# Two six-layer stacks: the last four bodies as one sequence with the turns of the results inside, and a shorter list of entry work

## The reference

```
x = x + 0.5 * _L2_ffn_ref(_layernorm(x), Wqkv, q_scale, k_scale, Wo, ln_g, ln_b, W1, b1, W2, b2)
x = x + _L2_attn_ref(_layernorm(x), ...)
x = x + 0.5 * _L2_ffn_ref(_layernorm(x), ...)

for layer in range(6):                       # _L2_ffn_ref, on z
    t = shift_tokens(z)                      # the upper 64 features come from the token before
    q, k, v = split(t @ Wqkv[layer])         # 16 heads of 64
    q, k = rotary(l2norm(q) * q_scale), rotary(l2norm(k) * k_scale)
    a = softmax(8 * q @ k.T over a window of 32 keys back) @ v
    z = z + a @ Wo[layer]
    n = layer_norm(z) * ln_g + ln_b
    z = z + (u * gelu(g)) @ W2 + b2          # u, g = split(n @ W1 + b1), 341 wide each
```

## Time and profile before

| | us |
|---|---|
| runs | 5355.53, 5368.52, 5376.36; median 5368.52 |
| the profiled execution | 5368.35, its span 5366.6 |
| first stack, entry to last x | about 1018 to 2768 |
| second stack | about 3004 to 4768 |
| from output(46) to output(47), first stack | 27.6 |
| from output(47) to the last x | 28.8 |

### The profile page before, as it was taken

One profiled execution on the slowest core, in us unless ns is written; L12 is line 12 of the kernel. 1 busy time (PEld: TensorE's weight loads), 2 busy tenths in 40 slices (PEclk: granted clock), 3 DMA queues, 4 the chain that ended last, 5 costly groups with the idle time before them and its releaser, 6 DMA issues. The chain is left out here.

```text
span 5366.6 us, 141783 instructions
## 1 busy us (share of the span) xinstructions
PE 4978.9 (93%) x49044; PEld 3454.0 (64%) x49044; DVE 3814.0 (71%) x7030; ACT 3438.1 (64%) x5879; POOL 2867.6 (53%) x3451
## 2 busy tenths in 40 slices
PE   8988977499999999999969699999999999989889
PEld 5655655267777777777745367777777777756556
DVE  2243236488888888888856488888888888845545
ACT  3333323278888888888845378888888888832642
POOL 0010005378788778778720288777787787700200
PEclk9989988599999999999979799999999999989899
DMA  1000000011111111112100111111111111110000
GB/s 44 1 5 34 1 1 9 29 45 55 51 50 51 55 51 49 51 51 55 43 15 1 40 39 55 51 51 49 55 51 55 46 55 51 39 34 7 1 25 9
DMA packets 110454, 195.51 MB, mean 36 GB/s; under 512 B 21409, under 2 KB 28849, under 8 KB 110257
## 3 DMA queue, kind: packets, MB, share of 16 engines
q1 hardware_dynamic: 110256, 192.82, 12.8%
HBM read 53.29 MB, written 1.05 MB: 10 GB/s over the span
## 5 line engine op out<-in xcount | busy, mean ns | idle before, releaser
L2674 POOL TENSOR_TENSOR stage_qk<-stage_halves 128x1024 f32<-128x1024 f32 x384 | 906.0, 2359 | 53.3 <-DVE stage_halves L2790 45.8
L2710 POOL TENSOR_TENSOR stage_qk<-stage_qk,stage_rnorm 128x1024 f32<-128x1024 f32 x384 | 730.9, 1903 | 30.5 <-issue 0.3
L2703 POOL TENSOR_TENSOR stage_probs<-stage_probs,stage_rsum 128x768 f32<-128x768 f32 x384 | 565.3, 1472 | 222.1 <-DVE stage_rsum L2819 209.6
L2787 DVE TENSOR_TENSOR stage_halves<-stage_wide,stage_tables 128x1024 f32<-128x1024 f32 x384 | 468.2, 1219 | 227.6 <-ACT stage_square L2493 187.4
L2493 ACT ACTIVATE stage_square<-stage_wide 128x1024 f32<-128x1024 f32 x384 | 394.0, 1026 | 191.9 <-PE stage_wide L2259 191.5
L2325 PE MATMUL stage_pv<-stage_probsT,stage_v_win 96*64 96x64 f32 x12288 | 488.1, 227 | 2.7 <-ACT stage_ctxT L2546 1.6
L2790 DVE TENSOR_TENSOR stage_halves<-stage_wide,stage_tables 128x512 f32<-128x512 f32 x768 | 490.5, 680 | 0.0
L2325 PEld LDWEIGHTS stage_pv<-stage_probsT,stage_v_win 96*64 96x64 f32 x12288 | 408.4, 137 | 122.7 <-issue 98.5
L2799 DVE TENSOR_REDUCE stage_norm<-stage_square 128x16 f32<-128x1024 f32 x384 | 464.7, 1210 | 30.8 <-issue 30.7
L2276 PE MATMUL stage_turn<-ident,stage_qk 128*128 128x128 f32 x3072 | 478.9, 279 | 4.9 <-ACT stage_qkT L2513 4.7
L2311 PEld LDWEIGHTS stage_flip<-ident,stage_probs 128*96 128x96 f32 x3072 | 355.6, 126 | 194.3 <-issue 130.0
(11 more groups left out here) (299 smaller groups left out, 9877.6 us busy)
## 6 DMA issues: line engine op xcount, KB each, us to landing
stage_v_win<-stage_v SPq DMA_DIRECT2D x384, 192.0 KB, 2.5
stage_v_win<-stage_v SPq DMA_DIRECT2D x384, 128.0 KB, 2.4
stage_v_win<-stage_v SPq DMA_DIRECT2D x192, 64.0 KB, 2.2
stage_wq<-in_T_wq SPq DMA_DIRECT2D x12, 512.0 KB, 4.1
stage_wk<-in_T_wk SPq DMA_DIRECT2D x12, 512.0 KB, 4.7
stage_wv<-in_T_wv SPq DMA_DIRECT2D x12, 512.0 KB, 3.5
stage_wo<-in_T_wo SPq DMA_DIRECT2D x12, 512.0 KB, 3.5
stage_w_up<-in_L_w_up SPq DMA_DIRECT2D x8, 512.0 KB, 6.6
```

What stands on the lines that cost most here:

```text
L2674: nc.gpsimd.tensor_tensor(qk[:, n, :], halves[:, n % 2, 0, :], halves[:, n % 2, 1, :], ALU.add)\
L2703: nc.gpsimd.tensor_tensor(probs[:, m % 2], probs[:, m % 2], rsum[:, m % 2].to_broadcast([P, 2, 2 * HALVES, REACH]), ALU.mult)\
L2710: nc.gpsimd.tensor_tensor(heads, heads, rnorm[:, n, :].rearrange("p (h o) -> p h o", o=1).to_broadcast([P, LH, LD]), ALU.mult).then_inc(at ...
L2787: nc.vector.tensor_tensor(out[:, 0], heads, cos.to_broadcast([P, LH, LD]), ALU.mult)
```

## The change

In the entry, v_win is set only in its first 32 rows of block 0 (32 x 1024, to 0.0), DVE makes only the table of layer 0, and the activation table for exp and ln is loaded at the head of the entry instead of the head of the main block. The tables of layers 1 to 5 are made by POOL at the head of its main list; DVE waits for them in front of its loop. At the end, the calls of `body` for 46 to 49 and the loop over the eight batches are replaced by one written list per engine, `tail()`, in which the parts of steps 45 to 47 stand in another order and the turns of the results between them: `straighten(b)` on ACT, `turn_out(b)` on PE, `leave(b)` on DVE. `straight` now lies in `square`, and the transposes go to the banks of `wide`.

```diff
-        straight = qk[:, 2, :].rearrange("p (a s) -> p a s", s=SEQ)
+        straight = square[:, 0, :].rearrange("p (a s) -> p a s", s=SEQ)
...
-                nc.gpsimd.memset(v_win[:, :, :, :], 1.0).then_inc(once["set"], 1)
+                nc.gpsimd.memset(v_win[0:WINDOW, 0, :, :], 0.0).then_inc(once["set"], 1)
...
             @block.scalar
             def _(act):
+                nc.scalar.preload_act_table_set("natural_log_exp_and_others")
...
-                for layer in range(DEPTH):
-                    table(layer)
-                dve.wait_ge(*once("tables", 1))
+                table(0)
+                dve.wait_ge(*once("tables", 0, 1))
...
+            def turn_out(b):
+                if b == 0:
+                    pe.wait_ge(*att("v", STEPS - 1, HALVES))
+                pe.wait_ge(att["leave"], att.base["leave"] + b + 1)
+                if b > 1:
+                    pe.wait_ge(att["left"], att.base["left"] + b - 1)
+                for t in range(HALVES):
+                    ins = nc.tensor.transpose(wide[:, b % 2, t * P:(t + 1) * P], straight[:, b % 4, t * P:(t + 1) * P], chip.ident[:, :])
+                ins.then_inc(att["tok"], 1)
...
+            def tail():
+                fourth, third, second, last = range(STEPS - 4, STEPS)
+                project(last, 5)
+                weigh(second, 0)
...
-            for s in range(STEPS - 2, STEPS + 2):
-                body(s)
-            for b in range(B):
...
+            tail()
...
+            def straighten(b):
+                if b == 0:
+                    act.wait_ge(*att("norm2", STEPS - 1, CHUNKS))
+                act.wait_ge(*att("z", STEPS + b + 1))
+                if b > 3:
+                    act.wait_ge(att["tok"], att.base["tok"] + B + b - 3)
+                nc.scalar.activation(straight[low, b % 4, :], z[low, b, 0:SEQ], ACT.Copy)
+                nc.scalar.activation(straight[high, b % 4, :], z[high, b, 1:SEQ + 1], ACT.Copy).then_inc(att["leave"], 1)
...
+            for layer in range(1, DEPTH):
+                nc.gpsimd.tensor_tensor(tables[:, layer], base[:, :, :, :], rows[:, layer].to_broadcast([P, 4, HALVES, LD]), ALU.mult)\
+                  .then_inc(once["tables"], 1)
...
+            def leave(b):
+                dve.wait_ge(att["tok"], att.base["tok"] + B + b + 1)
+                x = chip.x[:, b * HALVES:(b + 1) * HALVES, :]
+                nc.vector.scalar_tensor_tensor(x, tiles2(wide[:, b % 2, :]), 0.5, x, ALU.mult, ALU.add).then_inc(att["left"], 1)
...
             for s in range(-2, 2):
                 body(s)
+            dve.wait_ge(*once("tables", 1))
             att.settle(dve)
             with dve.Fori(2, STEPS - 2) as s:
                 body(s)
```

More of the change, by code:

```diff
@@ L2470, in _ @@
                 body(s)
-            for s in range(STEPS - 2, STEPS + 2):
-                body(s)
-            for b in range(B):
-                pe.wait_ge(att["leave"], att.base["leave"] + b + 1)
-                if b > 1:
-                    pe.wait_ge(att["left"], att.base["left"] + b - 1)
-                bank = (flip, turn)[b % 2]
-                for t in range(HALVES):
-                    ins = nc.tensor.transpose(bank[:, t * P:(t + 1) * P], straight[:, b % 4, t * P:(t + 1) * P], chip.ident[:, :])
-                ins.then_inc(att["tok"], 1)
+            tail()
         @block.scalar
```

216 lines of the change are left out of this document (200 added, 16 removed).

## The result

The changed kernel takes 5337.96 us (median of 9 runs, 5328.03 to 5348.02), the kernel before 5371.79 us (median of 9, 5354.6 to 5376.36): 33.8 us less, a ratio of 0.9945 with a 95% interval of 0.9932 to 0.9958. The forecast was 5332.8 us in a range of 5318 to 5348, so the time lies inside it, 5.2 us above the forecast. The profiled execution took 5331.61 us at a span of 5329.8, 36.8 us less than the span of before, with a mean granted clock of 0.953.

The account below looks back on a forecast made before the run. It saw PE with hardly a gap in the loop, the drain bound by engine-to-engine waits. Entry 5.7, drain 7.5, output(47) 1.8 and turns 2.8 make 17.8 us a stack, 35.6 off 5368.4: 5332.8 us, range 5318 to 5348.

Parts of the forecast that it names:

- Entry: Start of each stack: shorter memset, five tables on POOL and early table load bring xsT 5.7 us earlier.
- Drain (a): Up to output(46): the qkT copy moves earlier, so ctxT(46,3) starts as its weigh ends; 1.2 us won.
- Drain (b): Output(46) to the end of normalize(46): 10.4 us becomes 9.3, leave(3) and leave(4) counted at 0.42 each; 1.1 us won.
- Drain (c) and (d): Normalize(46) to end of gate(46,2)'s table load, 11.35 to 9.4, 1.9 us; then to output(47), 5.9 to 2.5, 3.4 us.
- Output(47): Output(47) itself in the drain: full clock instead of granted 0.69, 1.8 us won; other end 0.
- Its toss: Output(47)'s 1.8 us might not come, as the moment of a clock change varies from run to run.
- Turns: End of each stack: seven turns move inside the sequence and one stays behind the last z; 2.8 us won.
- Rival 1: Loop settles into another rhythm: both stacks slow 5342 us, chance 0.12; both fast 5323.6, chance 0.16 shared with clock up.
- Rival 2: Drain not shorter, some wait replacing (a) to (d): 5.7 + 2.8 us a stack, 5351.4 us; chance 0.12.
- Rival 3: PE stays at 2.4 GHz through the last feed-forward part: some 4 us less a stack, 5325; chance 0.16 shared with both fast.
- Rival 4: Clock falls for the drain: 19.6 us lost against 16.0 won a stack, 5375.6 us, slower than before; chance 0.03.
- Rival 5: Entry's tables on POOL late for the first sum: at most 5.9 us a stack lost, 5344.6 us; chance 0.04.

Follow-up runs that it names:

- the one with all fillers: Changed kernel plus needless identity transposes on TensorE, in larger sizes, in the entry, first two bodies and last feed-forward part: 5303.05 us, ratio 0.9870.

## Why the prediction was right, point by point

**Entry, 5.7 predicted, 5.87 and 5.84 measured.** Its steps stand: memset 0.94 where 0.88 was worked out, the DVE pair ended with it, ACT's last copy and not the table came last, POOL's tables cost 1.23 where 1.18 was taken and 1.82 us of cover were left. (Its price for a pair that isn't held, 6.5, is 6.3 by its own rows.) What the prediction lacked is a step behind it. It counted xsT(0) as time won for good, with the rest of the stack shifted as a block. The second step ran longer, by 2.0 us on the average, since the clock was lower in it. In these traces 0.51 and 1.40 us went between xsT(0) and xsT(47). It also credits the tables and the memset with parts of the gain that these traces don't show in the end: with either undone the total is within 0.7 us of the kernel after's, since the second step came out short in both.

**Drain (a), 1.2 predicted, 0.81 and 0.90 measured.** The term was right for the order alone. With the turns behind, 54.35 us in the first stack is 1.22 under before. The 0.41 us that the inner turns cost here weren't counted: the prediction put turns 0 to 5 at nothing.

**Drain (b), 1.1 predicted, 1.35 measured.** It charged leave(3) and leave(4) with 0.84 us. They lie where DVE waits for to_tokens anyway, and with the turns taken out the stretch is 0.03 shorter.

**Drain (c) and (d), 1.9 and 3.4 predicted, 1.45 and 3.30 measured.** With (b) that is 6.10 against 6.3 or 6.4, in the first stack. The three are read as intervals of two traces; no run moves one part of the order by itself. For the second the prediction took the first stack's row of before, although has a stretch of the second drain at half clock. There before had 30.29 us and 8.76 were won. In the old order four stacks gave 27.62, 27.63, 29.68 and 30.29; in the new one all 22 gave 21.50 to 21.54. The forecast should have set the mean of both stacks of before, 28.96, against the new order, not the faster one.

**Output(47), 1.8 predicted, 1.72 measured.** It ran at full clock in every stack of every kernel with the new order. The clock gave 0.40 back behind it: the next part took 18.92 us at 0.60 where it took 18.52 at 0.64. The prediction's "the 18.52 us stay as they are" was short by that. Its toss, for which it quoted the Trainium skill (TensorE: Matmul & The Clock Gate, What's actually happening), didn't come up in the new order: 3.72 us in 22 of 22 stacks. In the old one it did, with 5.41 us in three stacks and 3.72 in one, so the 1.72 are what these two traces show and not what the old order always cost. Where the clock's phase does vary from run to run is the second step, 31.1 to 34.6 us for the same code.

**Turns, 2.8 predicted, 2.80 and 2.79 measured,** and 2.8 lost again with the turns behind.

**Rivals.** Rival 1 fell: the rhythm of 34.44 and 34.65 us belongs to the first and the second stack in all thirteen kernels, with early or late entry. Rival 2 fell, no new wait took the old one's place. Rival 3 didn't happen in the kernel after, but its price of 4 us a stack was right: with the gaps filled in addition, output(47) to the last z went from 22.64 to 18.31 us. Rival 4 fell for the drain, at a clock of 1.00; its mechanism was alive at the other end of the stack, where nobody had put it, at 2 and not at 19.6 us. Rival 5 fell by 1.82 us.

So 35.6 us were predicted and 34.6 found in the stacks. The sum was right because two faults nearly cancelled: 2.4 us too little for the second drain, and 1.9 too much for the steps behind xsT(0). The rest, some 1.5 us, is mostly (a) and what followed output(47), in both stacks. That the two cancelled is luck: both hang on where the clock fell in the one execution traced of each kernel. The width of the forecast doesn't come out of the prediction's own bounds either: with 9.5 or nothing won in the drain and nothing at output(47), 5332.8 goes to 5328.8 or 5351.4, and not to 5322 or 5344.

## What to carry to other kernels

Before a start is made earlier, look at the clock behind it: a gain at the first instruction of a serial stretch counts only as far as it is still there where TensorE becomes the bound. Where the table by stage shows TensorE's own instructions on the chain at half clock beside gaps, filling these gaps with work that nobody waits for can be worth as much as a new order: here 11.8 and 16.1 us a stack in the traces, on top of 16.4 and 18.2 for the whole change. Small work that must be done anyway, such as the turns, can go into such gaps: seven of them cost 0.4 us there. And of a stretch with a varying clock take several rows, from each stack, ahead of setting the sum.

## What the runs showed of the hardware

Transposes of float32 data raised the clock. The entry has nothing else on TensorE until the priming of the scores. Ten microseconds of it, the kernel after and then the one with all fillers:

```profile
1018.40:1028.40 10.00, 4.80 (x14) 2.03 (x14) 8.59 (x46) 4.55 (x12) 5.35 (x8) 0.50 0.91 347
```

```profile
1024.00:1034.00 10.00, 6.90 (x44) 5.13 (x43) 8.59 (x46) 4.54 (x12) 5.24 (x8) 0.89 0.95 363
```

The clock goes from 0.50 to 0.89 on transposes alone. The Trainium skill (TensorE: Matmul & The Clock Gate, PE-mode transpose) says that in one kernel the full clock didn't engage for transpose mode. These float32 transposes didn't behave so, and for them the measurement decides; the rows call them MATMUL and don't show whether that mode was on. One of them took about 0.12 us at full clock (18 in 2.13 us).

The memset of 96 x 4096 takes 3.51 us on POOL and the one of 32 x 1024 takes 0.94, and a DVE pair of 0.60 us started beside them takes 3.57 and 1.01. POOL's tables beside DVE's rotations, which read PSUM and one SBUF operand, held neither: the rotation took 1.23 us against 1.22, and the last table, which ran beside it, took 1.26 us from its start to its end like the four before it.

The loop of the same code ran 34.44 us a step in the first stack and 34.65 in the second in every kernel, also where 91 more TensorE transposes stood ahead of it in the entry and the first body. So the way in which a stack begins doesn't set it. The cause stays open, at 9 us a run.
